# Reordering the last part of a four-group transformer kernel: earlier expert row sends, later shared downs, gathers and fetches in another order

## The chip, the cores and the metric

The kernel runs on one core of a Trainium2 chip. The metric is the time of one execution on the device in microseconds (us). The core has five queues that work independently: TensorE (PE, with its weight loads PEld), VectorE (DVE), ScalarE (ACT), GpSimd (POOL) and SyncE (SP). Each takes its own instructions strictly in order and waits at semaphores for the others.

## The reference

A block of two layers on 16 sequences of 128 tokens, 256 wide:

```python
x = x + tanh(g_xattn[0]) * wkv_scan(layernorm(x), ctx)                 # layer 0
x = x + tanh(g_ffn[0]) * (silu(h @ gate_w) * (h @ up_w) @ down_w
                          + product_key_experts(h))   # top 8 of 512 experts, h = layernorm(x)
x = x + tanh(g_xattn[1]) * linear_attention(layernorm(x), ctx)         # layer 1, 16 heads, gated
x = x + tanh(g_ffn[1]) * (routed(layernorm(x))        # each token goes to 2 of 8 experts, width 128
                          + shared(layernorm(x)))     # one expert for all tokens
```

Only the last line and what feeds it is touched by the change. `routed` scales each token's row by its score, sends it through the two chosen experts and adds both results to the token; `shared` is one more expert of the same shape.

## The kernel before, in words

The tokens are worked on in four main groups of four tiles (a tile is one sequence, 128 tokens). The order of all work is written out by hand as a list of steps, `SCHED`. An item "moe 2 0 1" is step kind `moe`, group 2, parts 0 and 1. Every engine walks through the same list and issues only its own instructions of each step. So the list sets the order on each engine, and semaphores tie the engines together. `START` opens the list, then come the parts 1 to 13 of `mlp f` for each of the four groups (one MLP or product-key unit each), with the items of `PLAN[("mlp", f)][part]` behind each part, and then `LAST`. In part p of `mlp`, TensorE makes the up products of unit p - 1 and the down products (L666) of unit p - 4; "mlp 3 14 15" are the last two downs.

The steps that the change moves, all of the layer 1 part:

- `attn g p`: attention of main group g. Parts 9 and 10 are the output product (L904) and VectorE's residual addition (L1224).
- `moe_in g 0 1 2`: moments of the layernorm on VectorE (L1198) and the reciprocal root on GpSimd (L1621), the normalization on VectorE (L1220), the transposes on TensorE. `attn_in` is the same for attention (its part 2 splits the transposed rows into a high and a low half on ScalarE and VectorE).
- `peer_in 3 0`: the transposed routing weights of the product-key experts. VectorE's last instruction of it (L1381, `exps_t_l`) is what TensorE's first spread matmul of the ninth unit (L732) waits for, in part 9.
- `moe g 0`: gate scores (L915 on TensorE, L1102 on ScalarE, then some 12 small VectorE instructions down to `row_bias`, L1478). `moe g 1`: the up products of the shared expert (L924), ScalarE's silu of the first and VectorE's product (L1486).
- `place g 0`: TensorE counts the tokens of each expert (L934) once `row_bias` is there. `place g 1 2`: VectorE works out each row's slot in the sorted order (from L1505) and the owner of each block of 128 rows (to L1547).
- `rows g t`: ScalarE scales tile t's rows into a buffer, twice (L1137, L1138). `send g t`: GpSimd scatters them to `x_rows` in HBM by indirect DMA (L1660), two per tile, once the slots are ready.
- `shared g 0`: the down product of the shared expert (L678, 8 matmuls per group). `shared g 1`: VectorE adds it to `x_nat` (L1224, two instructions).
- `load`, `blk 0 n`: the expert blocks in pairs, software-pipelined: SP loads pair n + 3, TensorE transposes pair n (L689), multiplies pair n - 1 by the experts' ups (L705), transposes the hidden rows of pair n - 2 (L715) and multiplies pair n - 3 by the downs (L724); ScalarE evicts; GpSimd scatters the results to `y_rows` (L1668). Pairs 0 to 15 hold the rows of main groups 0 to 2, pairs 16 to 23 those of group 3. VectorE copies the home addresses of the pairs ahead (in blk 0 those of pairs 0 and 1) once these are loaded.
- `fetch 0 q`: SP fetches two tiles' results of groups 0 to 2 from `y_rows`, after the scatters of pairs 0 to 15 have landed. `gather 0 q`: VectorE adds them to the output (L1569, L1570) and SP stores it. `fetch_tile`, `gather_tile` are the same for the four tiles of main group 3, after the last scatter; SP and ScalarE issue the fetches.

Of the kernel before, what the change touches and what calls it, by code (L numbers as in the profile page):

```python
# [117 lines left out]
def steps(text):  # L118

    out = []  # L120
    for item in text.split(","):
        kind, g, *which = item.split()
        out += [(kind, int(g), int(part)) for part in which]
    return out
# [68 lines left out]
    },  # L193
}

LAST = """mlp_out 3 0, attn_in 3 0, shared 0 0 1, shared 1 0, shared 2 0, attn_in 3 1, shared 1 1, shared 2 1,
    attn_in 3 2, blk 0 0 1, attn 3 0 1 2 3, blk 0 2, attn 3 4 5 6 7, blk 0 3, attn 3 8, blk 0 4, attn 3 9 10, moe_in 3 0,
    blk 0 5, moe_in 3 1, blk 0 6, moe_in 3 2, blk 0 7, moe 3 0, blk 0 8, rows 3 12 13, place 3 0 1, rows 3 14,
    rows 3 15, send 3 12 13 14 15, blk 0 9, place 3 2, blk 0 10 11 12 13 14 15 16 17 18 19 20,
    fetch 0 0 1 2 3 4 5, blk 0 21, gather 0 0, blk 0 22, gather 0 1, blk 0 23, gather 0 2, blk 0 24, gather 0 3, blk 0 25,  # L200
    gather 0 4 5, blk 0 26, moe 3 1, shared 3 0 1, fetch_tile 1 0 1 2 3, gather_tile 1 0 1 2 3"""

SCHED = steps(START)
for f in range(NG):

    for part in range(1, MLP_UNITS + 2):
# [5 lines left out]
        if part in PLAN[("mlp", f)]:  # L212
            SCHED += steps(PLAN[("mlp", f)][part])
SCHED += steps(LAST)

# [1633 lines left out]
```

How the kernel before makes its waits and increments, by code:

```python
        def full(eng, key):  # L507
            k, n = place[key]
            eng.wait_ge(bank_full[k], n)
            return ring[k]
# [1 line left out]
        def freed(eng, key):  # L513
            k, n = place[key]
            eng.wait_ge(bank_free[k], n)
# [1 line left out]
        def weigh_values(eng, g, c):  # L518
            ee_a, v = ee_a_of[g], v_of[g]
            eng.wait_ge(ctx_loaded[g], 16 * C)
            freed(eng, (("wkv_in", g), "T", c))
            va = ee_a[c][:, :, :].rearrange("p s (t j) -> p s t j", t=GT)[:, :, :, 1:]
            return eng.tensor_tensor(va[:, 0], va[:, 1], v[c][:, :].rearrange("p (t j) -> p t j", t=GT), ALU.mult)
# [36 lines left out]
        def hidden_made(eng, n):  # L561
            kind, f, u = ALL_UNITS[n]
            if ALL_UNITS[n] in HID_TURN:
                eng.wait_ge(hid_ready, HID_TURN[ALL_UNITS[n]])
            else:
                freed(eng, ((kind, f), "B", u))
# [1 line left out]
        def sent(eng, grp):  # L569
            for k in range(SENDS):
                done = sum(1 for g in range(GROUPS[grp][-1] + 1) for n in range(2 * GT) if (g * 2 * GT + n) % SENDS == k)
                eng.wait_ge(row_sent[k], 16 * done)
# [1 line left out]
        def y_done(eng, n):  # L575
            for k in range(RESULTS):
                blocks = sum(pair_blocks(m) for m in range(k, n, RESULTS))
                if blocks:
                    eng.wait_ge(y_sent[k], 16 * blocks)
# [20 lines left out]
        def xt_wait(eng, n):  # L601
            if n > 0:
                k, turn = place[last_xt_read[n - 1]]
                eng.wait_ge(bank_full[k], turn)
```

## Time and profile before

| | |
|---|---|
| time, median of 3 runs | 510.68 us (510.35 to 511.2) |
| the profiled execution | 510.63 us, its span 508.8 us |
| granted TensorE clock, mean | 0.964 of full speed |
| TensorE busy | 444.7 us (87%) |
| VectorE busy | 357.5 us (70%) |
| ScalarE busy | 245.0 us (48%) |
| GpSimd busy | 156.8 us (31%) |

The span runs from the first to the last instruction that the profiler recorded; what lies around it makes up the rest of the execution's time. A busy share is an average over all stages: which engine sets the pace differs from stage to stage.

### The profile page before, as it was taken

The page shows a single profiled execution, that of the slowest core. Times are in us where ns is not written, and L with a number is a line of the kernel's source. Part 1 is how long each engine was busy: PE and PEld are TensorE (multiplying, and loading weights), DVE is VectorE, ACT ScalarE, POOL GpSimd, SP SyncE. Part 2 cuts the span into 40 slices and gives each one's busy share as a digit, 9 for nine tenths or more (in the row PEclk, how much of TensorE's full clock was granted, in tenths as well). Part 3 has the DMA queues.
Part 4 walks back from the last instruction along what each step waited for, and adds up shares of the span by engine and source line. Part 5 has one row for each costly group of instructions (what it writes and reads, how often), then busy time and mean ns, then how long its engine had stood idle before and what let it go on. Part 6 is the DMA issues. An engine that isn't in the chain of part 4 may idle for free. (4 is left out here: it accounts for less than half of the span.)

```text
span 508.8 us, 7205 instructions
## 1 busy us (share of the span) xinstructions
PE 444.7 (87%) x2130; PEld 353.8 (70%) x2130; DVE 357.5 (70%) x1026; ACT 245.0 (48%) x453; POOL 156.8 (31%) x157
## 2 busy tenths in 40 slices
PE   1517999599999999999999999898998899899990
PEld 1315678467678877888778787787776688788860
DVE  6996669998577986585987967978778454621173
ACT  3608666355295355337044417270651644955540
POOL 3965324240002221100000000050426015477771
PEclk9965999799999999999999999999999999999996
DMA  8510222000200001950000000132323323346394
GB/s 299 199 32 16 63 88 64 21 1 0 96 9 0 2 0 57 308 145 0 2 0 1 1 1 1 32 102 76 120 87 101 108 81 114 104 145 196 107 386 138
DMA packets 32965, 42.00 MB, mean 83 GB/s; under 512 B 3483, under 2 KB 26781, under 8 KB 32928
## 3 DMA queue, kind: packets, MB, share of 16 engines
q1 hardware_dynamic: 28224, 32.28, 21.3%
q0 software_dynamic: 3744, 8.42, 4.5%
q10 hardware_dynamic: 960, 0.86, 0.5%
q8 instruction: 18, 0.29, 0.2%
q14 instruction: 19, 0.16, 0.1%
HBM read 24.97 MB, written 18.39 MB: 85 GB/s over the span
## 5 line engine op out<-in xcount | busy, mean ns | idle before, releaser
L666 PE MATMUL acc<-w_down,act_s 128*128 128x256 f32 x384 | 90.8, 383 | 0.9 <-DVE act_s L1406 0.9
L666 PEld LDWEIGHTS acc<-w_down,act_s 128*128 128x128 f32 x384 | 73.6, 192 | 12.6 <-DVE act_s L1406 1.3
L642 PE MATMUL ring<-xt_h,up_l 128*128 128x512 f32 x160 | 70.5, 440 | 2.9 <-DVE xt_l L1376 1.5
L1621 POOL TENSOR_TENSOR rstd<-var_eps,minus_half 128x4 f32<-128x4 f32 x14 | 14.9, 1067 | 171.4 <-DVE var_eps L1205 171.4
L644 PE MATMUL ring<-xt_h,up_h 128*128 128x512 f32 x160 | 64.1, 401 | 0.0
L643 PE MATMUL ring<-xt_l,up_h 128*128 128x512 f32 x160 | 64.1, 401 | 0.0
L1117 ACT ACTIVATE act_s<-ring 128x512 f32<-128x512 f32 x48 | 28.6, 596 | 69.1 <-PE ring L644 68.9
L705 PE MATMUL ring<-up_e,act_s 128*128 x184 | 44.2, 382 | 2.3 <-issue 2.1
L1660 POOL DMA_INDIRECT x_rows<-main_a,slots x32 | 31.0, 970 | 43.7 <-ACT main_a L1138 34.8
L637 PE MATMUL ring<-small,xn 128*128 128x128 f32 x144 | 21.7, 300 | 25.5 <-ACT xn L1009 13.3
L1410 DVE TENSOR_TENSOR act_s<-ring,act_s 128x512 f32<-128x512 f32 x32 | 22.0, 686 | 30.4 <-PE ring L644 19.0
L637 PEld LDWEIGHTS ring<-small,xn 128*128 128x128 f32 x144 | 18.3, 154 | 28.8 <-ACT xn L1009 14.1
L705 PEld LDWEIGHTS ring<-up_e,act_s 128*128 128x128 f32 x184 | 33.1, 191 | 6.9 <-issue 3.2
L642 PEld LDWEIGHTS ring<-xt_h,up_l 128*128 128x128 f32 x160 | 30.7, 192 | 10.3 <-DVE xt_l L1376 1.8
L644 PEld LDWEIGHTS ring<-xt_h,up_h 128*128 128x128 f32 x160 | 30.7, 192 | 7.4
L643 PEld LDWEIGHTS ring<-xt_l,up_h 128*128 128x128 f32 x160 | 30.8, 192 | 6.9 <-issue 1.2
L1117 ACT ACT_TABLE_LOAD x21 | 26.9, 1283 | 0.4
L1668 POOL DMA_INDIRECT y_rows<-act_s,block_home x16 | 16.9, 1057 | 29.9 <-ACT act_s L1175 25.5
L1198 DVE BATCH_NORM_STATS2 stats<-x_nat 128x6 f32<-128x256 f32 x64 | 22.4, 412 | 4.6 <-DMA x_nat<-in_x 4.2
L1224 DVE SCALAR_TENSOR_TENSOR x_nat<-ring,small,x_nat 128x512 f32<-128x512 f32 x24 | 18.0, 750 | 10.3 <-PE ring L904 7.7
L1563 DVE TENSOR_TENSOR pairs<-ring,pairs 128x256 f32<-128x256 f32 x12 | 5.1, 423 | 23.3 <-ACT pairs L1158 23.2
L1268 DVE RECIPROCAL main_a<-main_a 128x256 f32<-128x256 f32 x12 | 20.2, 1724 | 1.3 <-POOL main_a L1630 1.2
(277 smaller groups left out, 978.0 us busy)
## 6 DMA issues: line engine op xcount, KB each, us to landing
main_b<-x_rows SPq DMA_DIRECT2D x22, 257.0 KB, 3.0
x_rows<-v_t SPq DMA_DIRECT2D x1, 3983.5 KB, 16.0
up_l<-y_rows SPq DMA_DIRECT2D x5, 512.0 KB, 6.4
stage<-in_w_mlp SPq DMA_DIRECT2D x8, 256.0 KB, 2.6
up_e<-in_w_moe SPq DMA_DIRECT2D x8, 256.0 KB, 2.6
x_rows<-v_t SPq DMA_DIRECT2D x1, 1927.5 KB, 22.2
x_nat<-in_x SPq DMA_DIRECT2D x7, 256.0 KB, 7.5
out_x<-x_nat SPq DMA_DIRECT2D x6, 256.0 KB, 5.6
```

The source lines that it names most:

```text
L637: last = pe.transpose(bank[:, t * P:(t + 1) * P], xn[n % 2][:, t, c * P:(c + 1) * P], ident)
L642: pe.matmul(out, wl, xh, start=first, stop=False, skip_group_check=True)
L643: pe.matmul(out, wh, xl, start=False, stop=False, skip_group_check=True)
L644: return pe.matmul(out, wh, xh, start=False, stop=final, skip_group_check=True)
L666: last = pe.matmul(acc[t // 2][:, t % 2, :], act_s[n % RING][:, tok], w_down[:, u, :], start=u == 0 and t % 2 == 0, stop=final, skip_group ...
L705: last = pe.matmul(bank[:, j * 2 * P:(j + 1) * 2 * P], x_block_t[n % 2][:, c, j * P:(j + 1) * P], up_e[:, bass.ds(e * UP + c * 2 * P, 2 * ...
L1117: act.activation(act_s[n % RING][:, :], bank[:, :], ACT.Silu).then_inc(free_sem((step, "A", u)), 1)
L1198: last = dve.bn_stats(stats[:, n, t, :], x_nat[:, b, :])
L1224: return dve.scalar_tensor_tensor(out, bank, gates[:, gate:gate + 1], out, ALU.mult, ALU.add)
L1268: last = dve.reciprocal(den, den)
L1410: free((step, "B", u), dve.tensor_tensor(s[:, :], bank[:, :], s[:, :], ALU.mult))
L1660: pool.indirect_dma_start(x_rows[group_of(g)], bass.IndirectOffsetOnAxis(ap=slots[:, t, k:k + 1], axis=0), to_send[n % SENDS], None).then_ ...
```

## The change

Steps change their place in the list; none is added, removed or altered. In the last MLP group, attn 2 10 and moe_in 2 0 move to part 7, ahead of place 1; the rest of moe_in 2 moves one part ahead; moe 2 0 moves to part 10 and place 2 0 1 comes behind it there, while moe 2 1 stays in part 11; the rows and sends of main group 2 are listed one part sooner. In `LAST`, shared 1 and shared 2 move from the front to behind blk 26, attn_in 3 1 and attn_in 3 2 come behind blk 0 and blk 1, gather 2 to 5 move from between the last blocks to behind blk 26, and the fetches of the last tiles stand ahead of shared 3 1 and gather 4 5.

```diff
         4: "attn 2 0 1 2 3, rows 0 0, send 0 0, route 3 6",
         5: "attn 2 4 5 6 7, rows 0 1 2, send 0 1 2, route 3 7",
         6: "route 3 8, attn 2 8, rows 0 3, send 0 3",
-        7: "attn 2 9, place 1 0 1 2",
-        8: "attn 2 10, peer_in 3 0, moe_in 2 0, rows 1 4 5, send 1 4 5",
-        9: "moe_in 2 1, rows 1 6, send 1 6",
-        10: "moe_in 2 2, rows 1 7, send 1 7",
-        11: "moe 2 0 1, place 2 0 1 2",
-        12: "rows 2 8 9 10, send 2 8 9 10",
-        13: "mlp 3 14 15, rows 2 11, send 2 11, load 0 0 1 2",
+        7: "attn 2 9 10, moe_in 2 0, place 1 0 1 2",
+        8: "moe_in 2 1, peer_in 3 0, rows 1 4 5, send 1 4 5",
+        9: "moe_in 2 2, rows 1 6, send 1 6",
+        10: "moe 2 0, rows 1 7, send 1 7, place 2 0 1",
+        11: "moe 2 1, place 2 2, rows 2 8 9, send 2 8 9",
+        12: "rows 2 10 11, send 2 10 11",
+        13: "mlp 3 14 15, load 0 0 1 2",
     },
 }
 
-LAST = """mlp_out 3 0, attn_in 3 0, shared 0 0 1, shared 1 0, shared 2 0, attn_in 3 1, shared 1 1, shared 2 1,
-    attn_in 3 2, blk 0 0 1, attn 3 0 1 2 3, blk 0 2, attn 3 4 5 6 7, blk 0 3, attn 3 8, blk 0 4, attn 3 9 10, moe_in 3 0,
-    blk 0 5, moe_in 3 1, blk 0 6, moe_in 3 2, blk 0 7, moe 3 0, blk 0 8, rows 3 12 13, place 3 0 1, rows 3 14,
-    rows 3 15, send 3 12 13 14 15, blk 0 9, place 3 2, blk 0 10 11 12 13 14 15 16 17 18 19 20,
-    fetch 0 0 1 2 3 4 5, blk 0 21, gather 0 0, blk 0 22, gather 0 1, blk 0 23, gather 0 2, blk 0 24, gather 0 3, blk 0 25,
-    gather 0 4 5, blk 0 26, moe 3 1, shared 3 0 1, fetch_tile 1 0 1 2 3, gather_tile 1 0 1 2 3"""
+LAST = """mlp_out 3 0, attn_in 3 0, shared 0 0 1, blk 0 0, attn_in 3 1, blk 0 1, attn_in 3 2, attn 3 0 1 2 3, blk 0 2,
+    attn 3 4 5 6 7, blk 0 3, attn 3 8, blk 0 4, attn 3 9 10, moe_in 3 0, blk 0 5, moe_in 3 1, blk 0 6, moe_in 3 2, blk 0 7,
+    moe 3 0, blk 0 8, rows 3 12 13, place 3 0 1, rows 3 14, rows 3 15, send 3 12 13 14 15, blk 0 9, place 3 2,
+    blk 0 10 11 12 13 14 15 16 17 18 19 20, fetch 0 0 1 2 3 4 5, blk 0 21, gather 0 0, blk 0 22, gather 0 1, blk 0 23 24 25 26,
+    moe 3 1, shared 1 0, shared 2 0, shared 1 1, gather 0 2 3, shared 2 1, shared 3 0, fetch_tile 1 0 1 2 3, shared 3 1,
+    gather 0 4 5, gather_tile 1 0 1 2 3"""
```

## Rows read from the trace of the kernel before

**Rows 1.** The page, busy tenths of TensorE in 40 equal slices of the span.

```profile
PE   1517999599999999999999999898998899899990
```

**Rows 2.** Timeline, seam to the blocks: start, duration, engine, instructions, idle before and releaser.

```profile
380.72 0.96 POOL L1660 DMA_INDIRECT x_rows<-main_a,slots  x1 [8.53 <-ACT main_a L1138]
...
387.29 5.34 PE L678 MATMUL ring<-stage,kv_sum 128*128 128x256 f32 x24
...
389.57 0.96 POOL L1660 DMA_INDIRECT x_rows<-main_a,slots  x1 [0.30 <-issue]
...
396.67 0.66 PE L689 MATMUL ring<-small,main_b 128*128 128x128 f32 x4 [0.60 <-DMA main_b<-x_rows]
...
398.40 1.99 PE L705 MATMUL ring<-up_e,act_s 128*128 x8 [1.07 <-issue]
...
400.04 0.58 PE L642 MATMUL ring<-ax_h,qg_l 128*128 128x512 f32 x1
```

**Rows 3.** Timeline of the end, from 490 us.

```profile
490.50 0.69 DVE L1569 TENSOR_TENSOR x_nat<-x_nat,up_l 128x512 f32<-128x512 f32 x1 [0.27 <-DMA up_l<-y_rows]
490.64 3.60 PE L924 MATMUL ring<-xt_f_pad,stage 128*128 128x512 f32 x8
490.67 1.38 POOL L1668 DMA_INDIRECT y_rows<-v_t,block_home  x1 [0.30 <-issue]
...
494.34 0.69 DVE L1486 TENSOR_TENSOR kv_sum<-ring,kv_sum 128x512 f32<-128x512 f32 x1 [0.75 <-PE ring L924]
...
496.40 1.61 DVE L1224 SCALAR_TENSOR_TENSOR x_nat<-ring,small,x_nat 128x512 f32<-128x512 f32 x2 [1.36 <-PE ring L678]
...
497.90 0.98 POOL L1668 DMA_INDIRECT y_rows<-kv_sum,block_home  x1 [0.30 <-issue]
...
503.43 0.43 DVE L1575 TENSOR_TENSOR x_nat<-x_nat,gate_pad 128x256 f32<-128x256 f32 x1 [5.42 <-DMA gate_pad<-y_rows]
```

**Rows 4.** Timeline, parts 7 to 10 of mlp 3, TensorE, VectorE and GpSimd.

```profile
348.14 1.97 PE L904 MATMUL ring<-wo,q_pad 128*128 128x256 f32 x8 [1.32 <-DVE q_pad L1446]
...
351.01 0.22 DVE L1505 TENSOR_TENSOR_SCAN kv_sum<-later,ring 128x32 f32<-128x32 f32 x1
...
356.18 0.18 DVE L1547 TENSOR_TENSOR owner<-owner 1x31 f32<-1x31 f32 x1
...
358.36 0.69 DVE L1381 TENSOR_TENSOR exps_t_l<-ring,exps_t_h 73x512 fp32r<-73x512 f32 x1 [0.48 <-ACT exps_t_h L1109]
...
359.14 0.47 PE L732 MATMUL ring<-exps_t_l,sel_exps 128*128 128x512 f32 x1 [0.28 <-issue]
...
361.06 1.04 POOL L1621 TENSOR_TENSOR rstd<-var_eps,minus_half 128x4 f32<-128x4 f32 x1 [16.26 <-DVE var_eps L1205]
...
361.91 0.58 PE L642 MATMUL ring<-xt_h,up_l 128*128 128x512 f32 x1
...
363.64 1.38 DVE L1220 TENSOR_SCALAR xn<-x_nat,mv,rstd 128x256 f32<-128x256 f32 x4
```

**Rows 5.** Timeline, TensorE in the same unit of main group 0.

```profile
98.80 0.77 PE L732 MATMUL ring<-exps_t_l,sel_exps 128*128 128x512 f32 x1 [5.26 <-DVE exps_t_l L1381]
...
103.94 1.88 PE L772 MATMUL ring<-wkv,v_odd 128*128 128x512 f32 x4
```

**Rows 6.** Windows: length, PE, PEld, DVE, ACT, POOL busy, granted clock, DMA share, GB/s.

```profile
95.00:98.00 3.00, 0.00 (x0) 0.00 (x0) 2.98 (x3) 0.00 (x0) 1.31 (x1) 0.75 0.00 0
98.00:101.00 3.00, 2.20 (x5) 1.52 (x6) 2.95 (x3) 0.91 (x3) 0.00 (x0) 0.50 0.00 0
```

**Rows 7.** Timeline, part 11 of mlp 3: moe 2 and the count matmul.

```profile
370.60 1.85 PE L915 MATMUL ring<-later,xt_f_pad 128*128 128x8 f32 x16
...
372.31 3.68 PE L924 MATMUL ring<-xt_f_pad,stage 128*128 128x512 f32 x8
...
376.13 0.30 PEld L934 LDWEIGHTS ring<-wanted,later 128*128 128x128 f32 x2 [0.97 <-DVE row_bias L1478]
```

**Rows 8.** Waits of TensorE, 340 to 400: total, times, longest.

```profile
PE acc L666 <- DVE act_s L1406: 0.9, 1, 0.9
```

## The prediction

> **What bounds the kernel now.** I read the page first. Its row of busy tenths for TensorE [rows 1] stands at 8 or 9 in nearly all slices from the fifth to the next to last: TensorE's own queue sets the pace of the middle of the kernel, and whatever makes it wait there delays all that follows. Then I read the timeline of the last 160 us, engine by engine, for the places where something else leads.
>
> At the seam between the last MLP group and the expert blocks, the eight row sends of main group 2 lead [rows 2]. GpSimd issues them 1.26 us apart, the first at 380.72, the last at 389.57. The rows have to land before the loads of the first pairs start, and TensorE reaches the second pair's transposes at 396.67, 7.1 us after the last send, released by that load. It had filled the time with the 24 shared down matmuls of three groups (387.29, 5.34 us). The first expert matmuls start at 398.40 and attn 3 0 at 400.04, right behind them.
>
> At the end GpSimd leads [rows 3]. Its last y_rows scatter is issued at 497.90 and is over at 498.88; the fetched tiles reach VectorE at 503.43, while VectorE has been idle since 498.0. TensorE had begun moe 3 1 (L924) at 490.64. I call that start S: it shifts as the whole block stage shifts, and VectorE's tile additions begin at S + 12.8.
>
> **Part 7 to 9 of mlp 3: the transposed routing weights come late.** VectorE works in the order of the list. Today place 1 1 and 1 2 run from 351.01 to 356.36 (5.35 us) and exps_t_l, the last step of peer_in 3 0, ends at 359.05; TensorE's first spread matmul (L732) starts at 359.14 without having lost more than 0.3 us [rows 4]. After the change VectorE first waits for all 16 matmuls of attn 2 9 10, begun at 348.14 and over near 351.8, adds the second residual (0.8, to 352.6), makes the moments of moe_in 2 0 (359.05 to 361.06 today, so 2.0, to 354.6), then place 1 1 and 1 2 (5.35, to 360.0), the unit's product (0.7, to 360.7), the normalization that now stands ahead of peer_in (1.38, to 362.1) and exps_t_l (0.69, to 362.8). TensorE has the same work ahead of this point as today and gets there at about the same time, so L732 starts at 362.9 in place of 359.14: **+3.8 us**, with TensorE idle all that time. Queued behind it are the rest of the unit, down, and the transposes of moe_in 2.
>
> That such a wait is real shows in main group 0, where exps_t_l was late in the same way: TensorE stood 5.26 us before L732 at 98.80 [rows 5]. The granted clock fell meanwhile, from 1.00 to 0.50 (2.4 to 1.2 GHz), with a mean of 0.75 in 95 to 98, and stayed low for some us after the work came back [rows 6]. From that L732 to the end of the unit's down the time was 98.80 to 103.94, 5.14 us; the same sequence at the full clock took 359.14 to 361.91, 2.77 us [rows 4, 5]. A fall costs **2.4 us**.
>
> The Trainium skill has this as a rule (TensorE: Matmul & The Clock Gate, section on the HAM clock gate): the array's clock is halved while it idles and is given back only after sustained work. The trace agrees, with 0.50 behind the 5.26 us wait. By the page's rule the two waits of this change would each be followed by slow matmuls; without it the total below would be 518.5, which is also the rival without a fall.
>
> **Part 10: the count matmul has nothing to stand behind.** Today moe 2 0 and moe 2 1 follow each other. The gate matmuls (L915) start at 370.60 and take 1.85 us, the shared matmuls (L924) fill 372.31 to about 375.9, and the counting matmul of place 2 0 starts at 376.13, released by VectorE's row_bias [rows 7]: 3.7 us of routing arithmetic on ScalarE and VectorE, covered. After the change moe 2 1 stands one part later and place 2 0 comes straight behind moe 2 0 (the rows and sends between are ScalarE's and GpSimd's). The same 3.7 us is then bare: **+3.7 us**. It is long enough for a second fall of the clock.
>
> Where is the send then? The gate matmuls stand one unit sooner in the queue. A unit takes 3.9 us (361.91 to 370.60, less 0.9 for the transposes, is two units) [rows 4, 7]. Gained 3.9, lost 3.8: place 2 0 starts at 376.0 as today. ScalarE's row copies, though, now stand behind the silu of moe 2 1, and TensorE needs a unit (3.9) and the first half of moe 2 1 (1.85) to get there: 376.0 + 0.5 + 3.9 + 1.85, plus an estimated 1.2 for the silu and the first row (ScalarE's steps taken like VectorE's 0.69 for 512 columns [rows 3]), is 383.4. The slots, which follow the count matmul as today, are there by 380.7. So the first send goes at 383.4, not 380.72, and the last at 392.2: **+2.6 us**, for a step that was moved a part ahead. TensorE itself ends its downs later by 3.8 + 3.7 less the 0.9 it lost before the last down today [rows 8], because VectorE has place 2 behind it by then: 6.6 later, near 393.8. Then shared 0 (1.8) and it idles.
>
> **LAST: attn_in 3 behind the first pair loads.** The two shared groups taken out here (16 of the 24 matmuls, 3.6 us) buy nothing: the second pair arrives at 396.67 + 2.6 = 399.3, and TensorE waits for it. But attn_in 3 1 now stands behind blk 0, whose VectorE step copies the addresses of pairs 0 and 1 and so waits for that load. The normalization ends at 399.3 + 0.3 (my estimate for the copies) + 1.4 = 401.0, the expert matmuls run 401.0 to 402.7, then come eight transposes (1.1 by the four in 0.66 [rows 2]) and the split into high and low halves, which the trace before always shows covered. Its cost is between nothing and 2.7 (four steps of about 0.69 in a row); with the first half done while the other is transposed I take 1.6. Attn 3 0 starts at 405.4, not 400.04: **+5.4 us**, which holds the +2.6 of the sends.
>
> The order from there to S is the old one, without slack on TensorE, so S shifts by 5.4, and by 2 x 2.4 for the two falls (each delays TensorE's parts 9 to 11 and through them the first send): **10.1 to 10.2 us**, S = 500.8.
>
> **The end.** VectorE's product of moe 3 1 ends at S + 4.4 in both kernels. Today one shared residual pair (1.6) follows, and it waits for the fetch. After the change three pairs (4.8) and four gathers (two additions of 0.69 each, 5.6) come ahead of the tiles, the first pair ending at S + 6.5: 6.5 + 2.8 + 1.6 + 1.6 + 2.8 = S + 15.3, against S + 12.8: **+2.5 us**. GpSimd would allow the tiles sooner. It shifts by 10.1, and gains up to 1.5 us because its scatters take 1.35 us instead of 0.98 while VectorE's gather additions run [rows 3] and four of the six now run behind it: last scatter over at 507.5, tiles there at 512.0, VectorE ready at 516.1. The fetches that SP issues stand behind the store of gather 3 (S + 9.3, 510.1) and land near 514: still hidden.
>
> The sum, against the profiled execution: span 508.8 + 10.1 + 2.5 = 521.4, and 1.8 around it (510.63 less 508.8): **523.2 us**. That execution is 0.05 below the median of the runs, 510.68.
>
> **Rivals.**
> The clock falls only once or not at all: 520.9 or 518.5. For it: the waits are 3.7 to 3.8 us, shorter than the 5.26 us that was followed by the fall. Against it: a mean of 0.75 over 95 to 98 puts that fall near 96.5, 3 us into a wait that began at 93.5 [rows 5, 6]. Chance 0.18.
> A third fall: TensorE, free at 395.6 plus the falls, has only transposes until the expert matmuls, some 5 us later. Today's idle time there is broken by attn_in's transposes and the clock held. 523.2 + 2.4 = 525.6. Chance 0.15.
> GpSimd still ends the kernel, VectorE's queue being quicker than I count: 510.6 + 10.1 - 1.5 = 519.2. Chance 0.08. (The Trainium skill, SBUF — State Buffer, Who interferes with whom, infers that additions with both inputs in SBUF leave descriptor generation alone; the scatter at 1.38 beside 0.98 speaks against it. By the page GpSimd gains nothing and this rival is 520.7.)
> The waits on TensorE turn out covered, the sends gain 3.9 us, but attn_in 3 waits for the load: -3.9 + 2.7 + 2.5, 512.0. Chance 0.06.
> Faster: the sends lead everything to the end. Place: the first send, at 376.8 instead of 380.72, with attn_in 3 ready in time. Price: S sooner by 3.9, less the 2.5 of VectorE's end, 509.2. It decides once attn 3 0 starts more than 3.5 us sooner, before 396.5. For it: rows 2, where the sends lead today. Against it: it needs place 2 0 not to wait. Chance 0.09.
> No change to be told, between these: 0.03.
>
> **How the numbers follow.** The forecast has 0.41, and its own range is 521 to 525 by the bounds of the split and of a fall. All cases with the two waits bare give 518.5 to 525.6, 0.82 together. The range 515 to 526 takes these in, with some room for a wait smaller than worked out; below it lie the covered cases, 0.18. The spread of the runs is 510.35 to 511.2, so about 0.2% (1.0 us) can be told from no change: faster 0.09, same 0.03, slower 0.88.
>
> **What would show it.** The waits of TensorE should list L732 behind exps_t_l and L934 behind row_bias with 3 to 4 us each, and the granted clock should fall near both. The first send of main 2 should be at 383 or later (386 to 388 with the falls), attn 3 0 near 410, L924 of moe 3 1 near 501, and the tile additions should follow VectorE's own work instead of a wait for a DMA. I am wrong if TensorE shows no wait at L934, if the first send comes before 380, or if the tiles still wait for the fetch.

## The result, and the profile after

The changed kernel takes 526.71 us (median of 4 runs, 524.68 to 528.21), the kernel before beside it 510.94 (510.35 to 511.7): ratio 1.0298, interval 1.0277 to 1.032. It is slower, 15.8 us by the medians. The forecast was 523.2, so the sign was right and the size 3.5 us short, 0.7 above the range. The profiled execution of the changed kernel took 528.21, with a span of 526.4; all stretches below add up to that one, 17.6 over the span before. It is the slowest of the four runs, 1.5 above their median.

**The page.** TensorE's busy tenths and the clock granted to it, in 40 slices of 13.2 us. First after, then the clock line of before:

```profile
PE   1518999699999999999999998986796899899991
...
PEclk9956999799999999999999999997789799999997
```
```profile
PEclk9965999799999999999999999999999999999996
```

Against [rows 1] TensorE's new dips are in slices 28, 29 and 31 (6, 7 and 6, from 355 us on), and the clock line, which stands at 9 all through there before, shows 7, 7, 8, 9, 7 in slices 28 to 32, 355 to 421 us. So one looks at that stretch for waits and for falls of the clock.

**Waits of TensorE, 340 to 415 us, after** (total, times, longest), and under them the longest of before, 340 to 400:

```profile
PE ring L732 <- issue: 4.2, 1, 4.2
PE ring L689 <- issue: 4.0, 1, 4.0
PE ring L934 <- DVE row_bias L1478: 3.9, 1, 3.9
```
```profile
PE ring L904 <- DVE q_pad L1446: 1.3, 1, 1.3
```

Three waits of some 4 us, where the longest one before was 1.3. The 0.9 of [rows 8] was only the fourth longest there.

**Timeline, parts 7 to 11 of mlp 3, after:**

```profile
348.01 3.69 PE L904 MATMUL ring<-wo,q_pad 128*128 128x256 f32 x16 [1.32 <-DVE q_pad L1446]
...
359.76 0.18 DVE L1547 TENSOR_TENSOR owner<-owner 1x31 f32<-1x31 f32 x1
...
360.70 1.51 DVE L1220 TENSOR_SCALAR xn<-x_nat,mv,rstd 128x256 f32<-128x256 f32 x4
...
362.14 0.68 DVE L1381 TENSOR_TENSOR exps_t_l<-ring,exps_t_h 73x512 fp32r<-73x512 f32 x1
...
362.92 0.77 PE L732 MATMUL ring<-exps_t_l,sel_exps 128*128 128x512 f32 x1 [4.18 <-issue]
...
368.62 1.26 PE L637 MATMUL ring<-small,xn 128*128 128x128 f32 x8
...
379.32 0.64 PE L934 MATMUL ring<-wanted,later 128*128 128x32 f32 x2 [3.93 <-DVE row_bias L1478]
...
386.89 3.60 PE L924 MATMUL ring<-xt_f_pad,stage 128*128 128x512 f32 x8
...
389.39 0.59 ACT L1138 ACTIVATE main_a<-x_nat,row_bias,row_scale 128x256 f32<-128x256 f32 x1
...
390.77 0.95 POOL L1660 DMA_INDIRECT x_rows<-main_a,slots  x1 [11.56 <-ACT main_a L1138]
```

"issue" beside L732 means that the trace names no releaser; the timeline does: exps_t_l ends at 362.82 and L732 starts 0.1 later, behind the whole of place 1 and the normalization (L1220). Counted from the output product L904, L732 stands at 14.91 after and 11.00 before [rows 4], 3.9 later. The count matmul L934, which had followed the shared ups within a few tenths [rows 7], now waits 3.93 for row_bias. The first row send of main group 2 is at 390.77, against 380.72 [rows 2].

**Granted clock in windows of the same stretch and the next, after** (columns as in [rows 6]):

```profile
360.00:362.00 2.00, 0.00 (x0) 0.00 (x0) 1.96 (x5) 0.94 (x2) 1.50 (x2) 1.00 0.21 68
362.00:364.00 2.00, 1.08 (x3) 0.59 (x4) 0.82 (x2) 0.00 (x0) 1.58 (x2) 0.56 0.36 130
...
376.00:378.00 2.00, 0.00 (x0) 0.00 (x0) 1.83 (x16) 1.98 (x4) 0.96 (x1) 0.50 0.56 211
382.00:384.00 2.00, 2.00 (x6) 1.24 (x5) 1.70 (x9) 0.60 (x1) 0.00 (x0) 0.50 0.00 0
...
406.00:408.00 2.00, 0.94 (x6) 0.70 (x5) 0.67 (x3) 0.60 (x1) 0.00 (x0) 0.66 0.98 322
410.00:412.00 2.00, 2.00 (x7) 1.55 (x6) 0.00 (x0) 0.00 (x0) 0.00 (x0) 0.50 0.32 100
```

1.00 is 2.4 GHz and 0.50 is 1.2 GHz. Each of the three waits of 3.9 to 4.2 us is followed by busy TensorE time at 0.50 (the third wait is shown in the next timeline). That is three falls, not two. The 0.50 stands even in 376 to 378, where TensorE idles.

**Timeline of the seam, after:**

```profile
399.78 1.89 PE L678 MATMUL ring<-stage,kv_sum 128*128 128x256 f32 x8
...
405.66 0.63 PE L689 MATMUL ring<-small,main_b 128*128 128x128 f32 x4 [3.99 <-issue]
...
407.33 0.17 DVE L1554 COPY block_home<-main_b 128x2 uint32<-128x2 uint32 x1 [1.50 <-DMA main_b<-x_rows]
407.35 1.11 PE L689 MATMUL ring<-small,main_b 128*128 128x128 f32 x4 [1.06 <-DMA main_b<-x_rows]
407.41 1.38 DVE L1220 TENSOR_SCALAR xn<-x_nat,mv,rstd 128x256 f32<-128x256 f32 x4
409.25 3.78 PE L705 MATMUL ring<-up_e,act_s 128*128 x8 [0.78 <-issue]
...
415.79 0.47 PE L642 MATMUL ring<-ax_h,qg_l 128*128 128x512 f32 x1 [1.62 <-DVE ax_l L1369]
```

The shared downs (L678, 8 in place of 24) end at 401.67. TensorE then has nothing for 4 us, until the first pair arrives. Attention's normalization (L1220) starts only when the second pair has landed, behind the address copy (L1554). The expert matmuls L705 take 3.78 us, against 1.99 [rows 2], at 0.50. Attn 3 0 starts 6.54 after L705 instead of 1.64.

**Timeline of the end, after:**

```profile
506.33 3.60 PE L924 MATMUL ring<-xt_f_pad,stage 128*128 128x512 f32 x8
...
512.23 0.99 POOL L1668 DMA_INDIRECT y_rows<-kv_sum,block_home  x1 [0.30 <-issue]
515.22 3.10 DVE L1224 SCALAR_TENSOR_TENSOR x_nat<-ring,small,x_nat 128x512 f32<-128x512 f32 x4
...
521.02 0.42 DVE L1575 TENSOR_TENSOR x_nat<-x_nat,gate_pad 128x256 f32<-128x256 f32 x1
```

Moe 3 1 (L924) starts at S = 506.33, 15.7 later than in [rows 3]. The tile additions (L1575) start at S + 14.69 with no wait in front of them; before it was S + 12.79 behind 5.42 us of waiting for a DMA. 15.7 + 1.9 = 17.6, the whole difference of the spans.

### The profile page after: what moved, and what is told of

Same layout as the page of the kernel before. It is cut to its first block and busy times, and to the rows that moved or that the text cites. A ratio compares the mean times of both kernels' runs of the same rounds, so it can differ in the third digit from the quotient of the medians.

```text
span 526.4 us, 7207 instructions
## 1 busy us (share of the span) xinstructions
PE 452.3 (86%) x2130; PEld 359.3 (68%) x2130; DVE 358.1 (68%) x1026; ACT 245.2 (47%) x453; POOL 155.3 (30%) x157
## 5 line engine op out<-in xcount | busy, mean ns | idle before, releaser
L666 PE MATMUL acc<-w_down,act_s 128*128 128x256 f32 x384 | 93.0, 390 | 0.0
L666 PEld LDWEIGHTS acc<-w_down,act_s 128*128 128x128 f32 x384 | 75.4, 197 | 12.3
L642 PE MATMUL ring<-xt_h,up_l 128*128 128x512 f32 x160 | 71.2, 445 | 2.9 <-DVE xt_l L1376 1.5
L705 PE MATMUL ring<-up_e,act_s 128*128 x184 | 46.0, 393 | 2.0 <-issue 1.8
L637 PE MATMUL ring<-small,xn 128*128 128x128 f32 x144 | 22.2, 305 | 24.4 <-ACT xn L1009 13.3
L705 PEld LDWEIGHTS ring<-up_e,act_s 128*128 128x128 f32 x184 | 34.2, 196 | 7.2 <-issue 3.2
L642 PEld LDWEIGHTS ring<-xt_h,up_l 128*128 128x128 f32 x160 | 31.0, 193 | 10.6 <-DVE xt_l L1376 1.8
L637 PEld LDWEIGHTS ring<-small,xn 128*128 128x128 f32 x144 | 19.1, 159 | 27.8 <-ACT xn L1009 14.1
L1224 DVE SCALAR_TENSOR_TENSOR x_nat<-ring,small,x_nat 128x512 f32<-128x512 f32 x24 | 18.0, 750 | 10.1 <-PE ring L904 8.7
L732 PE MATMUL ring<-exps_t_l,sel_exps 128*128 128x512 f32 x24 | 14.5, 604 | 10.0 <-DVE exps_t_l L1381 5.3
## 6 DMA issues: line engine op xcount, KB each, us to landing
x_rows<-v_t SPq DMA_DIRECT2D x1, 3983.5 KB, 17.6
```

The lines of the kernel that those rows point to most:

```text
L637: last = pe.transpose(bank[:, t * P:(t + 1) * P], xn[n % 2][:, t, c * P:(c + 1) * P], ident)
L642: pe.matmul(out, wl, xh, start=first, stop=False, skip_group_check=True)
L666: last = pe.matmul(acc[t // 2][:, t % 2, :], act_s[n % RING][:, tok], w_down[:, u, :], start=u == 0 and t % 2 == 0, stop=final, skip_group ...
L705: last = pe.matmul(bank[:, j * 2 * P:(j + 1) * 2 * P], x_block_t[n % 2][:, c, j * P:(j + 1) * P], up_e[:, bass.ds(e * UP + c * 2 * P, 2 * ...
L1224: return dve.scalar_tensor_tensor(out, bank, gates[:, gate:gate + 1], out, ALU.mult, ALU.add)
```

## The experiments

All kernels below compute the whole reference. Where matmuls are added as fillers, they write into a PSUM bank that the waiting step has just opened and overwrites before it is read. "Tile" is the start of the tile additions counted from the start of L904 in part 7, in the profiled execution: a length that holds every part of the change and leaves out what differs ahead of it. The kernels ran on several chips, so each has its own runs of before beside it. The ratio and its interval are worked out over these runs side by side, and are not the quotient of the two medians.

| kernel | median us (range, runs) | before, same chip | ratio (interval) | Tile, us |
|---|---|---|---|---|
| before | 510.94 (510.35 to 511.7, 4) | | | 155.29 |
| after | 526.71 (524.68 to 528.21, 4) | 510.94 | 1.0298 (1.0277 to 1.032) | 173.01 |
| e1_plan_only | 520.67 (519.34 to 520.85, 4) | 511.02 | 1.0174 (1.014 to 1.0208) | 165.98 |
| e2_last_only | 517.66 (516.94 to 518.37, 4) | 511.02 | 1.0118 (1.0086 to 1.015) | 163.27 |
| e3_kept_busy | 521.02 (518.79 to 522.06, 4) | 511.02 | 1.0176 (1.0134 to 1.0217) | 165.61 |
| e4_covered | 516.24 (515.72 to 517.16, 4) | 511.02 | 1.0101 (1.0069 to 1.0133) | 161.51 |
| e5_attn_in_first | 513.39 (512.78 to 513.79, 4) | 511.23 | 1.0048 (1.0032 to 1.0065) | 157.84 |
| e6_late_gathers | 510.72 (509.92 to 511.62, 10) | 511.23 | 0.9995 (0.9983 to 1.0007) | 156.17 |
| e7_one_filled | 524.05 (523.9 to 525.27, 4) | 511.23 | 1.0264 (1.0247 to 1.0282) | 169.02 |
| e8_covered_old_last | 509.30 (508.37 to 510.69, 10) | 511.23 | 0.9963 (0.9949 to 0.9977) | 154.37 |
| e9_last_filled | 516.08 (514.68 to 516.66, 4) | 511.78 | 1.0072 (1.0049 to 1.0095) | 161.08 |
| e10_third_filled | 525.06 (524.06 to 525.23, 4) | 511.78 | 1.0251 (1.0232 to 1.027) | 170.18 |
| e11_kept_busy_4 | 518.88 (518.23 to 519.3, 4) | 511.78 | 1.0134 (1.0116 to 1.0152) | 164.31 |

The theory was: two or three bare waits on TensorE, a fall of the clock behind each, and the late attn_in. The main rivals: the waits alone carry the whole loss and the clock is only a companion, or the seam's new order alone does it.

**e1_plan_only and e2_last_only: the two halves of the change.** The first has the new list of mlp 3 and the old last part, the second the reverse.

```diff
 # e1_plan_only                                  # e2_last_only
-        7: "attn 2 9, place 1 0 1 2",           (PLAN as before)
+        7: "attn 2 9 10, moe_in 2 0, place 1 0 1 2",
 ...
 LAST as before                                  LAST as after
```

> The new order inside mlp 3 with the old LAST. Theory (TensorE's two bare waits and the clock falls behind them carry most of the loss): TensorE ends its downs 12.5 us later as in the changed kernel, the first send goes 10 us later, but attn_in 3 is ready when the first pairs arrive and the three shared downs keep the clock up; attn 3 0 some 11 us later than before, GpSimd ends the kernel as before, 521.7 us. Rival (the new LAST carries most of it): 510.7 plus at most 4, under 515.

> The old order inside mlp 3 with the new LAST. Theory: attn_in 3 waits for the second pair's load (+2.9), TensorE idles some 6 us ahead of the blocks, its clock falls (+2.2), and VectorE's queue ends the kernel 1.9 later: 515.5 to 517.7 us. Rival (the shared downs taken out of the seam are a gain, the loss is in mlp 3 alone): 509 or less.

By the medians the halves cost 9.65 and 6.64 us, 16.3 together beside 15.8 for the whole: they add up, and neither hides the other. The first send of e1 is at 390.03 and L705 has its 1.99 us again: with the 24 shared downs in front of the pairs the clock does not fall at the seam, though the sends are as late as in the whole change. In e2 the sends are as before (380.50), and the seam reads:

```profile
397.65 1.12 PE L689 MATMUL ring<-small,main_b 128*128 128x128 f32 x4 [1.47 <-DMA main_b<-x_rows]
399.56 3.78 PE L705 MATMUL ring<-up_e,act_s 128*128 x8 [0.78 <-issue]
...
405.93 0.47 PE L642 MATMUL ring<-ax_h,qg_l 128*128 128x512 f32 x1 [1.62 <-DVE ax_l L1369]
```

So the third fall belongs to the new last part: taking 16 shared downs out of the front of it leaves TensorE idle for 6.1 us ahead of the first pair (its longest wait in this stretch).

**e3_kept_busy and e11_kept_busy_4: the waits stay, the clock is held.** The whole change, with fillers ahead of the three waits; e11 adds four ahead of the count matmul of main group 3.

```diff
+            def keep_busy(bank, n):
+                for _ in range(n):
+                    pe.matmul(bank[:, :], qg_h[:, 0, 0:P], qg_l[:, 0, :], start=True, stop=True, skip_group_check=True)
...
     # ahead of the wait of the ninth unit's spread, main group 3
+    keep_busy(bank, 16)
...
     # ahead of the count matmul, g == 2 (e11: also g == 3, with 4)
+    keep_busy(bank, 15)
     pe.wait_ge(chosen_ready, g + 1)
...
     # ahead of the transposes of pairs 0 and 1
+    keep_busy(bank, (16, 4)[n])
     pe.wait_ge(blocks_loaded[n % 4], 16 * (n // 4 + 1))
```

> The changed kernel with TensorE kept at work in its three waits: 16 dummy matmuls into the bank that is opened anyway, ahead of the wait before the spread of the ninth unit, 15 ahead of the count matmul of place 2, 16 and 4 ahead of the first two pairs' transposes. The waits and the order stay. Theory (the falls of the clock cost 3.2, 3.2 and 2.2 us beside the waits): granted clock 1.00 throughout, 518.1 us, and runs as close together as those of the kernel before. Rival (the falls lie beside other waits and cost little): 524 or more. If the dummies outlast a wait, up to 1 us comes on top.

> As the run with TensorE kept at work in its three waits (521.02 us), and 4 dummies ahead of the count matmul of place 3, where TensorE waits 0.9 us and the profile showed a fourth fall, to 0.5 near 447 to 450. Theory (that chance fall is what was left of the miss): the clock holds, 518.5 to 519 us with a narrower spread. Rival (something else in the dummies costs 2 us): 521.

e3 missed its expectation, 521.02 for 518.1. Its three places did hold, and a fall came somewhere else. Windows of e3, then its timeline at main group 3's place step:

```profile
362.00:364.00 2.00, 1.41 (x5) 0.88 (x6) 0.62 (x2) 0.43 (x1) 1.70 (x2) 1.00 0.38 134
376.00:378.00 2.00, 1.78 (x10) 1.50 (x10) 1.10 (x8) 0.00 (x0) 0.12 (x1) 1.00 0.19 66
...
446.00:448.00 2.00, 1.42 (x6) 1.04 (x4) 1.75 (x11) 2.00 (x8) 1.70 (x2) 0.74 0.25 23
448.00:450.00 2.00, 2.00 (x6) 1.55 (x6) 1.40 (x7) 2.00 (x8) 0.39 (x2) 0.50 0.61 215
```
```profile
445.15 0.39 PE L947 MATMUL ring<-wanted,later 128*128 128x32 f32 x2 [0.89 <-DVE row_bias L1491]
...
446.80 3.65 PE L707 MATMUL ring<-up_e,act_s 128*128 x8 [0.58 <-issue]
```

Only two short waits, 0.89 and 0.58, stand around that fall, and before and after held the clock there. With four fillers at that place e11 comes to 518.88, within its expectation, and its four runs lie within 1.1 us. Holding the clock gives back 7.8 us by the medians (8.4 by the ratios, 8.7 by Tile). The ratios and Tile weigh more here, because the two medians come from different chips. What is left over before, 7.1 against e11's own runs of before (6.9 by the ratio, 9.0 by Tile), are waits and order. The rival that the clock is only a companion has fallen: about half of the loss is the clock's.

**e7_one_filled and e10_third_filled: one fall at a time.** The whole change with 15 fillers ahead of the count matmul of main group 2 alone, and with 16 and 4 ahead of pairs 0 and 1 alone (the lines above).

> The changed kernel with 15 dummy matmuls ahead of the count matmul of place 2 alone. Theory: the fall of the clock in that wait is gone, those in the first and third wait stay; 3.2 us less than the changed kernel, 523.5 us. Rival (the three falls are one state of the chip, all gone or all there): 518 to 519, or 526.7.

> The changed kernel with dummies ahead of the first two pairs' transposes alone (16 and 4). Theory (the third fall costs 2 us, the other two stay): 524.5 us. Rival (the third fall lies beside other waits): 526.7.

By the medians 2.7 and 1.65 us less than the whole change, by the ratios 1.7 and 2.4; Tile is 4.0 and 2.8 shorter. The first fall was not run by itself. What is left for it is 3.5 by the medians (7.8 - 2.7 - 1.65), 4.3 by the ratios and 1.9 by Tile. So the share of a single fall is known only to 1 or 2 us: the ratio intervals of e7 and of the whole change even touch.

**e9_last_filled: the third fall alone, without the other two.** e2 with 24 and 5 fillers ahead of pairs 0 and 1.

> The run with the old mlp 3 and the new LAST (517.66 us), with 24 and 5 dummy matmuls ahead of the waits for the loads of the first two pairs. Theory (its loss is 2.8 for attn_in behind the load, 1.9 at the end, and the rest a fall of the clock in the 6 us wait): the fall goes, 515.5 to 516 us. Rival (TensorE's emptiness at the seam costs nothing by itself): 517.7.

1.6 us less than e2 by the medians, 2.4 by the ratios and 2.2 by Tile. L705 takes 1.99 again, and attn 3 0 starts 4.49 after it instead of 6.37: 1.9 us were the fall's. Before it was 1.64, so attn_in's place costs 2.8 with the clock held (e10 and e11 have 4.48). The 1.62 us of waiting for ax_l stay.

**e5_attn_in_first: the seam without attn_in behind the pair.** e2, with the last two steps of attn_in ahead of the first block step.

```diff
-LAST = """mlp_out 3 0, attn_in 3 0, shared 0 0 1, blk 0 0, attn_in 3 1, blk 0 1, attn_in 3 2, attn 3 0 1 2 3, ...
+LAST = """mlp_out 3 0, attn_in 3 0, shared 0 0 1, attn_in 3 1, attn_in 3 2, blk 0 0 1, attn 3 0 1 2 3, ...
```

> The run with the old mlp 3 and the new LAST (517.66 us), with attn_in 3 1 and attn_in 3 2 put back ahead of blk 0. Theory (their place behind the load of the second pair costs 2.8 us, and TensorE's idle time loses the other part by the clock): attn 3 0 starts right behind the first expert matmuls, 2.8 us or more sooner relative to them; shared 1 and 2 stay at the end, so TensorE still idles before the transposes and its clock may fall: 513 to 515 us. Rival (the order of attn_in does not matter): 517 or more.

4.3 us less than e2, from two steps put ahead of one. Timeline of e5, then a window of it:

```profile
393.85 1.97 PE L637 MATMUL ring<-small,xn 128*128 128x128 f32 x8 [4.70 <-DVE xn L1220]
...
398.90 1.99 PE L705 MATMUL ring<-up_e,act_s 128*128 x8 [1.15 <-issue]
400.53 0.58 PE L642 MATMUL ring<-ax_h,qg_l 128*128 128x512 f32 x1
...
491.22 3.60 PE L924 MATMUL ring<-xt_f_pad,stage 128*128 128x512 f32 x8
...
505.91 0.42 DVE L1575 TENSOR_TENSOR x_nat<-x_nat,gate_pad 128x256 f32<-128x256 f32 x1
```
```profile
394.00:396.00 2.00, 2.00 (x10) 2.00 (x11) 0.37 (x1) 0.75 (x2) 0.00 (x0) 0.50 0.79 223
```

Attention follows L705 as in [rows 2], and most of what remains is the end: the tiles at S + 14.69. The time is 2.2 us above before. The clock falls here too: with the 16 downs gone TensorE waits 4.70 us for the normalization and runs the transposes behind it at 0.50. But behind these it has to wait for the second pair anyway, and the clock is back at 1.00 by 398 us, before L705 starts. From L904 to S it is 143.15 us, against 142.50 before. So the clock falls once the downs are gone, wherever attn_in stands, and attn_in's place decides what the fall costs: about 2 us in e2, 0.65 at most in this profile.

**e6_late_gathers: the end's order alone.** The kernel before, with gathers 2 to 5 behind the last block and the tile fetches ahead of VectorE's shared 3 1; the shared downs stay at the seam.

```diff
-    ... blk 0 23, gather 0 2, blk 0 24, gather 0 3, blk 0 25, gather 0 4 5, blk 0 26, moe 3 1, shared 3 0 1, fetch_tile 1 0 1 2 3, ...
+    ... blk 0 23 24 25 26, moe 3 1, gather 0 2 3, shared 3 0, fetch_tile 1 0 1 2 3, shared 3 1, gather 0 4 5, ...
```

> The kernel before with only the end reordered: gather 2 to 5 behind blk 26 and the fetches of the last tiles ahead of shared 3 1; shared 1 and 2 stay in front. Theory (VectorE has room for the four gathers while GpSimd drains; only the two extra residual pairs make its queue too long): 510 to 511 us, no loss. If the additions of the gathers slow GpSimd's scatters, up to 0.7 us gained. Rival (gathers behind the blocks are themselves the loss at the end): 512.5.

No change that can be told: 0.9995, and the interval holds 1. In its profile the tiles start at S + 11.99, after a wait of 0.47 for the fetch, so the end is 0.8 shorter than before; 0.8 is within what the ratio's interval allows. The same profile had a fall at the seam, which hides that gain in it; more on this below. So the late gathers cost nothing by themselves; the 1.9 us at the end come with the two shared pairs (3.1 us of L1224) that stand in VectorE's queue as well.

**e4_covered: the waits covered by order.** The whole change, with peer_in 3 0 back ahead of place 1, and place 2 behind a whole unit.

```diff
-        7: "attn 2 9 10, moe_in 2 0, place 1 0 1 2",
-        8: "moe_in 2 1, peer_in 3 0, rows 1 4 5, send 1 4 5",
+        7: "attn 2 9 10, peer_in 3 0, moe_in 2 0, place 1 0 1 2",
+        8: "moe_in 2 1, rows 1 4 5, send 1 4 5",
...
-        10: "moe 2 0, rows 1 7, send 1 7, place 2 0 1",
-        11: "moe 2 1, place 2 2, rows 2 8 9, send 2 8 9",
+        10: "moe 2 0, rows 1 7, send 1 7",
+        11: "place 2 0 1, moe 2 1, place 2 2, rows 2 8 9, send 2 8 9",
```

> The changed kernel with both bare waits covered: peer_in 3 0 ahead of moe_in 2 0 and place 1 in part 7, and place 2 0 1 one part later, behind unit 10 and ahead of moe 2 1. The new LAST stays. Theory: the first send goes near 377, 4 us sooner than in the kernel before, attn_in 3 still waits for the second pair and VectorE's end stays 1.9 longer: 511.5 to 514 us. Rival (it is not those two places, the waits come back elsewhere): above 520.

10.5 us less than the whole change, and still 2.2 above its own expectation. The first send, which I had expected to gain a good part of a unit, is 31.65 after L904, against 32.58 before: VectorE takes the three operations of the tenth unit ahead of the slots, which release the send now. At the seam the wait of 5.05 us is still there and the clock falls behind it (L705 to attn 3 0 takes 6.84).

**e8_covered_old_last: the same list with the old front of the last part** and the end of e6.

> Both waits of mlp 3 covered as in the covered run, with the old front of LAST and the gathers late. Theory: the first send 1 us sooner than before, the clock up throughout, up to 0.7 us from the gathers: 509 to 510 us, a little faster than the kernel before. Rival (TensorE's 1.7 us wait for moe_in 2 takes the gain back): 511.

```profile
379.76 0.96 POOL L1660 DMA_INDIRECT x_rows<-main_a,slots  x1 [5.92 <-DVE slots L1529]
...
397.58 1.99 PE L705 MATMUL ring<-up_e,act_s 128*128 x8 [1.07 <-issue]
...
490.43 3.60 PE L924 MATMUL ring<-xt_f_pad,stage 128*128 128x512 f32 x8
...
502.45 0.43 DVE L1575 TENSOR_TENSOR x_nat<-x_nat,gate_pad 128x256 f32<-128x256 f32 x1 [0.51 <-DMA gate_pad<-y_rows]
```

509.30, faster than before by 0.37% (0.23 to 0.51). Tile is 0.9 shorter than before, 0.8 of it at the end (S + 12.02). The earlier send is worth almost nothing: of the 0.9 gained there 0.15 is left at S. How the gain divides between the list and the end was not settled, e6's own interval being too wide.

## Why the forecast had the sign right and the size short

**The late exps_t_l, step "Part 7 to 9": right.** Forecast +3.8, L732 at 362.9. Measured +3.9, 362.92.

**The bare count matmul, step "Part 10": right.** Forecast 3.7, measured 3.93. The forecast also had the send behind the silu of moe 2 1: GpSimd waits 11.56 us for ScalarE's row copy, not for the slots. From the start of L924 to the first send it counted 1.85 + 1.2 and the trace shows 3.88, 0.8 more (3.87 in e11). ScalarE was as quick as counted: its first row copy ends at 389.98, 3.09 after L924. But the send starts only 0.79 behind that copy (0.78 in e11), although the kernel lets it go with it. Behind VectorE's slots in e8 a send starts after 0.28. The forecast had nothing for this step, and what it is made of was not settled.

**"Where is the send then?": right in kind, too small.** Forecast +2.6 without the falls. In e11, where the clock holds, the first send stands 36.63 after L904, against 32.58 before: +4.05. Of the 1.4 missing, 0.8 are this step and 0.5 the count matmul, which stood at 376.5 by the same count and not at 376.0.

**The falls, step "A fall costs 2.4 us" and the sum "2 x 2.4 for the two falls": this is the step that failed,** in number and in size. I priced a fall from one instance [rows 5] and counted two. There the clock came back within the downs behind it (L666 3.00 us); in the first fall after, they took 3.62. In the profile after there are three. From L732 to what follows the unit (now the transposes L637) it is 5.70 us, against 2.77 to L642 [rows 4]: 2.9. From L934 to L924 it is 7.57 us, against 4.4 (0.5 for the count and a unit of 3.9): 3.2. At the seam attn 3 0 starts 6.54 after L705, and 4.48 after it in e10, where the same wait is filled: 2.1. Together 8.2 where the forecast had 4.8. The chip's own answer is e11, in which the waits are filled and the clock does not fall: 7.8 us by the medians, 8.4 by the ratios, 8.7 by Tile, for 4.8.

**The third fall was a rival with 0.15.** I set against it that today's idle time at this place is broken by attn_in's transposes. But the same change moves these transposes behind the pair load, and takes out 16 of the 24 shared downs; both were worked out a few lines above. The wait was foreseen (TensorE free at 395.6 plus the falls, expert matmuls some 5 us later) and only its consequence was discounted. e2 shows the fall without the other two, e1 the seam without it. e5 parts the two causes: with the transposes back ahead of the load the clock falls all the same, so they alone had not held it. With all 24 downs in front it holds in the profiles of before, e1 and e8, though not in that of e6.

**attn_in behind the first pair, step "LAST": right.** The mechanism is in the timeline row by row: address copy at 407.33, normalization at 407.41, L642 waiting 1.62 for the low half (forecast 1.6). With the clock held (e9, e10, e11) attn 3 0 starts 4.48 to 4.49 after L705, against 1.64 before: 2.8, where the forecast had 2.7.

**The end: right.** Forecast +2.5, VectorE ready later than the tiles. Measured +1.9 and no wait for a DMA. VectorE's queue was 0.6 quicker than counted: the four shared instructions took 3.10 us in a row, not 3.2, and the gather additions ran without gaps. The scatters on GpSimd lay off the path.

**The sum.** Without falls the forecast was 7.8 us over before. e11 stands 7.1 over its own runs of before by the medians, 6.9 by the ratio, 9.0 by Tile. The stretches of the profile show that this near agreement is in part luck: from L904 to S e11 is 7.1 longer than before where the forecast had 5.4, and the end 1.9 where it had 2.5. For the whole change Tile is 17.7 longer and the forecast had 12.7. Of the 5.0 missing, 3.9 are the falls (8.7 for 4.8), 1.7 the way to S without them, 1.4 of it at the send, and the end takes back 0.6. The falls are most of the miss, and the send is the rest.

**The other rivals.** "The clock falls once or not at all" fell with the windows, "the waits turn out covered" with the list of waits, and "GpSimd still ends the kernel" with the end of the timeline. "The sends lead and gain" needed a place 2 0 that does not wait; e4 and e8 made one, and the send came 0.9 us sooner, not 3.9: the forecast had not asked what VectorE does ahead of the slots.

## What to carry to other kernels

When a step is moved forward in a list that all engines share, look for what had covered its cross-engine chain: here 3.7 us of routing arithmetic lay behind 3.7 us of matmuls, and moving it "one part sooner" sent the rows 10 us later. Price every bare wait on TensorE of some 4 us with the matmuls that follow at half clock as well, some 2 to 3 us here where they lay on the path and 0.65 at most where they stood ahead of another wait (e5). Count all such waits of the new order, also those whose filler the change itself takes away. If the order can't be mended, matmuls into the bank that is about to be used hold the clock (about half of the loss here), but the order without the waits was better still (e8, which also has the old front of the last part).

## What the runs showed of the hardware that was not expected

**The clock also falls where another profile of the same work holds it.** e3 lost the clock at 446 with waits of 0.89 and 0.58 around it. e6 has the same list as before up to the last gathers, but its profile fell at the seam, where the same windows of before show 1.00:

```profile
396.00:398.00 2.00, 0.92 (x6) 0.72 (x5) 1.26 (x5) 0.60 (x1) 0.00 (x0) 0.98 0.15 50
398.00:400.00 2.00, 2.00 (x7) 1.65 (x5) 0.00 (x0) 0.00 (x0) 0.00 (x0) 0.50 0.69 222
```

From L904 to S it is 144.18 us in e6, against 142.50 before. This is a likely source of the runs' spread. Only profiled executions show where a fall comes, but every run has a mean granted clock, and over 33 runs of before (509.73 to 513.47) the two slowest, 513.18 and 513.47, have the two lowest, 0.958 and 0.959, the others 0.961 to 0.968. What brings such a fall was not settled. Another part of the spread arises early: L904 of part 7 stands between 346.97 and 348.14 in the thirteen profiles, whose lists agree up to there, and the granted clock of 40 to 55 us was 0.79 in e9 (346.97) and 0.71 in before (348.14). There the clock comes back behind a TensorE that hardly worked from 35 to 40 us. The Trainium skill has something like it for a kernel's start (TensorE: Matmul & The Clock Gate, What's actually happening): how many of a kernel's first matmuls run slow differs from run to run. These rows show it in the middle of one; at the start, 10 to 20 us, both profiles have 1.00.

**A GpSimd scatter is slowed by a VectorE addition that starts together with it.** In [rows 3] the scatter that starts 0.17 after an L1569, whose two inputs lie in SBUF, takes 1.38 us instead of 0.98. In e2 two scatters have such a partner, and the third has none:

```profile
488.52 0.69 DVE L1569 TENSOR_TENSOR x_nat<-x_nat,up_l 128x512 f32<-128x512 f32 x1 [1.97 <-DMA up_l<-y_rows]
488.57 1.49 POOL L1668 DMA_INDIRECT y_rows<-act_s,block_home  x1 [0.30 <-issue]
...
490.25 0.68 DVE L1569 TENSOR_TENSOR x_nat<-x_nat,up_l 128x512 f32<-128x512 f32 x1
490.37 1.41 POOL L1668 DMA_INDIRECT y_rows<-act_s,block_home  x1 [0.31 <-issue]
...
492.09 0.99 POOL L1668 DMA_INDIRECT y_rows<-act_s,block_home  x1 [0.30 <-issue]
```

The Trainium skill (SBUF — State Buffer, Who interferes with whom) infers that an addition with both inputs in SBUF leaves the generation of descriptors alone; these rows disagree, by 0.4 to 0.5 us a scatter. It does not happen every time: in e4 a scatter at 485.92 beside an addition at 485.88 took 0.99, and there the addition took 0.77 instead of 0.69. What decides was not settled, and no experiment was made for it, since GpSimd did not set the end.
